# Router operations of a fused transformer block move from VectorE to GpSimd, with a softplus sum in halves and fills counted per unit

## The reference

```
h = layernorm(x) * (1 + ca) + sa
x = x + ga * A(h)          # A: attention (16 heads of 16) and a state-space scan side by side, then a feed-forward net
h = layernorm(x) * (1 + cb) + sb
x = x + gb * F(h)          # F: a linear layer plus routed LoRA experts
```

```
logits = x @ router_w.T + router_b                 # 8 experts
kth    = second largest logit
masked = where(logits < kth, -1e9, logits)
w      = softmax(masked)
out    = x @ base_w.T + base_b + 2.0 * sum_e w[e] * (x @ lora_A[e]) @ lora_B[e]
```

## Time and profile before

| | us |
|---|---|
| three runs | 5759.66, 5759.91, 5764.49 |
| median | 5759.91 |
| profiled execution, its own time | 5763.4 |
| its span, first to last instruction | 5761.6 |

### The profile page before, as it was taken

The page is one execution under the profiler, slowest core; times in us unless marked ns, Lnnn a source line. Parts: engine busy times, 40 slices in busy tenths (PEclk is TensorE's granted clock), DMA queues, the critical chain, the costliest instruction groups (busy, mean ns, idle before and its releaser), DMA issues.

```text
span 5761.6 us, 94560 instructions
## 1 busy us (share of the span) xinstructions
PE 5214.0 (90%) x32280; PEld 3490.0 (61%) x32280; DVE 5161.4 (90%) x7776; ACT 4082.5 (71%) x6407; POOL 4217.8 (73%) x2545
## 2 busy tenths in 40 slices
PE   4799998999999999999999999999999999999986
PEld 2466665666666566666566656666656666666664
DVE  4999999999999999999999999999999999999983
ACT  3777777767777777777777777777777777777763
POOL 3777777777777777777777777777777777777762
PEclk7899999999999999999999999999999999999998
DMA  4444445444444444444444445444454445554441
GB/s 127 145 146 140 146 143 147 146 148 133 151 136 153 143 145 140 145 142 154 142 143 138 142 150 151 143 138 143 143 155 147 142 139 146 143 151 145 140 128 39
DMA packets 521455, 812.22 MB, mean 141 GB/s; under 512 B 80432, under 2 KB 227288, under 8 KB 520976
## 3 DMA queue, kind: packets, MB, share of 16 engines
q1 hardware_dynamic: 513072, 805.79, 46.5%
q10 hardware_dynamic: 7904, 0.39, 0.1%
HBM read 716.50 MB, written 88.38 MB: 140 GB/s over the span
## 4 chain that ended last, share of the span: by engine, by line
PE 54%; DVE 22%; ACT 10%; issue 9%; DMA 1%; POOL 1%; SPq 1%; DVEq 0%; POOLq 0%; ACTq 0%
PE pY L931 8%; PE pM L1073 8%; PE pM L1082 7%; DVE pD L1192 6%; PE pM L953 4%; DVE state L1200 4%; PE pM L1062 4%; PE pM L1006 4%; DVE mx L1250 3%; PE pM L1037 3%; DVE xc L1232 3%; PE pM L1019 2%; PE pM L940 2%; PE pM L988 2%; DVE state L1192 2%
## 5 line engine op out<-in xcount | busy, mean ns | idle before, releaser
L575 POOL TENSOR_TENSOR state<-scan_in,bc 128x1024 f32<-128x1024 f32 x1024 | 2426.1, 2382 | 852.7 <-PE pY L931 603.1
L1192 DVE TENSOR_TENSOR_SCAN pD<-pD,state 128x512 f32<-128x512 f32 x1536 | 1830.0, 1215 | 111.9 <-ACT pD L699 96.8
L699 ACT ACTIVATE pD<-scan_in,A 128x512 f32<-128x512 f32 x2048 | 1391.7, 686 | 432.8 <-DVE state L1200 336.0
L931 PE MATMUL pY<-ident,state 128*128 128x128 f32 x8192 | 1180.7, 280 | 13.0 <-DVE state L1200 8.5
L931 PEld LDWEIGHTS pY<-ident,state 128*128 128x128 f32 x8192 | 934.9, 145 | 258.8 <-issue 178.3
L1200 DVE TENSOR_TENSOR state<-pD,bc 128x512 f32<-128x512 f32 x1536 | 1030.6, 682 | 23.6 <-DMA bc<-bc_d 8.7
L800 ACT ACTIVATE region<-pM 128x512 f32<-128x512 f32 (+1 forms) x1408 | 754.1, 555 | 329.6 <-PE pM L1039 303.9
L1250 DVE TENSOR_REDUCE mx<-pM 128x1 f32<-128x512 f32 (+3 forms) x1408 | 857.1, 628 | 122.0 <-PE pM L1021 119.5
L1037 PE MATMUL pM<-region 98*128 98x512 bf16 (+3 forms) x2048 | 559.8, 318 | 269.2 <-ACT region L800 149.8
L562 POOL TENSOR_TENSOR state<-state,bc 128x512 f32<-128x512 f32 x512 | 647.5, 1273 | 205.0 <-DVE state L1192 175.5
L1019 PE MATMUL pM<-region 96*128 96x512 bf16 (+3 forms) x2048 | 548.2, 305 | 92.9 <-DVE mx L1250 71.6
(11 more groups left out here) (171 smaller groups left out, 8359.8 us busy)
## 6 DMA issues: line engine op xcount, KB each, us to landing
bc<-bc_d SPq DMA_DIRECT2D x2048, 256.0 KB, 4.1
region<-qk_d SPq DMA_DIRECT2D x640, 128.0 KB, 3.6
qk_d<-qkp SPq DMA_DIRECT2D x64, 384.0 KB, 2.9
qk_d<-ht SPq DMA_DIRECT2D x64, 384.0 KB, 4.0
xt<-in_x_dram SPq DMA_DIRECT2D x32, 512.0 KB, 5.4
hres_d<-xt SPq DMA_DIRECT2D x32, 512.0 KB, 4.8
region<-qk_d SPq DMA_DIRECT2D x256, 64.0 KB, 3.1
x<-hres_d SPq DMA_DIRECT2D x32, 512.0 KB, 5.0
```

The source lines that it names most:

```text
L575: nc.gpsimd.tensor_tensor(state[:, at_:at_ + JP], us[:, parity(b), k // N * JP:(k // N + 1) * JP, :], bc[:, k % BC_SLOTS, 0, :].unsqueeze( ...
L699: act.activation(pD[DECAY_BANK[e]][:], dts[:, parity(b), j], ACT.Exp, scale=A[:, j, n:n + 1]).then_inc(a_ok.sem, 1)
L931: ins = pe.matmul(y_part(t, e % JP), state[:, e % RING, t * P:(t + 1) * P], ident[:], is_transpose=True, start=False, stop=(e % PASS >= PA ...
L1192: v.tensor_tensor_scan(h if e in POOL_C else decay, decay, h, 0.0, ALU.mult, ALU.add)\
```

## The change

1. **Router.** Three operations go to GpSimd as steps `route`, `wkeep` and `wnorm`, which stand behind `+ql2` and ahead of `fill18`: the subtraction of the largest logit (into a new tensor `lgs`), the product with `keep`, and the product with the reciprocal of the sum. The factor 2.0 goes into `lora_B` once, in the setup. `keep` stays on VectorE as four operations of 128x8 with the second largest logit as a scalar per partition. The sum and its reciprocal stay on VectorE as step `esum` between `scan31` and `lora`.
2. **Softplus sum** in halves, `sp3_0` and `sp3_1`, each with its count, so that `u0` waits for the first half only, and so does ScalarE's first decay.
3. **Fills** are counted per unit.
4. **Order of waits.** In `scan` the wait for the decay stands ahead of that for the fill; in `fill_states` that for TensorE comes first; ScalarE's `oe` waits for its buffer first; a second wait on the same semaphore in `mx` at its first step is gone.

Nothing else in the lists and in the placement of banks changes.

```diff
+        lgs = sb("lgs", [P, TB, E])
@@
-                    e = JP * last + JP - 1
                     if row == 0:
-                        before.wait(sp, b_ok, e + 1)
+                        before.wait(sp, b_ok, last + 1)
@@ fill_states
-                if k == 0:
-                    b.wait(pool, u_ok)
-                b.wait(pool, *row_in(b, k, 0))
-
                 if e >= RING:
                     b.wait(pool, y_ok, e + JP - RING)
                 else:
                     b.wait_last(pool, y_ok, SCANS + e + JP - RING)
+                if k % N == 0:
+                    b.wait(pool, u_ok, k // N + 1)
+                b.wait(pool, *row_in(b, k, 0))
...
-                                        ALU.mult).then_inc(b_ok.sem, JP)
+                                        ALU.mult).then_inc(b_ok.sem, 1)
@@ GpSimd
+                elif name == "route":
+                    b.wait(pool, rt_c)
+                    nc.gpsimd.tensor_tensor(lgs[:], lg[:], top[:, :, 0:1].broadcast_to([P, TB, E]), ALU.subtract)\
+                      .then_inc(rk_ok.sem, 1)
+                elif name == "wkeep":
+                    b.wait(pool, ex_ok)
+                    b.wait(pool, kp_ok)
+                    nc.gpsimd.tensor_tensor(ew[:], ew[:], keep[:], ALU.mult).then_inc(wk_ok.sem, 1)
+                elif name == "wnorm":
+                    b.wait(pool, es_ok)
+                    nc.gpsimd.tensor_tensor(ew[:], ew[:], esum[:].unsqueeze(2).broadcast_to([P, TB, E]), ALU.mult)\
+                      .then_inc(ew_ok.sem, 1)
@@ ScalarE, oe
-                    b.wait(act, pv_ok, (g + 1) * TB)
                     if g:
                         b.wait(act, ot_ps, g)
                     else:
                         b.wait_last(act, o_fin)
+                    b.wait(act, pv_ok, (g + 1) * TB)
@@ ScalarE, route2
-                    b.wait(act, rt_c)
-                    act.activation(ew[:], lg[:], ACT.Exp).then_inc(ex_ok.sem, 1)
+                    b.wait(act, rk_ok)
+                    b.wait(act, kp_ok)
+                    act.activation(ew[:], lgs[:], ACT.Exp).then_inc(ex_ok.sem, 1)
@@ VectorE
+            link(v.tensor_scalar(w_lb[:], w_lb[:], LORA_SCALE, None, ALU.mult))
@@ scan
-                b.wait(dve, b_ok, e + 1)
                 b.wait(dve, a_ok, e + 1)
+                b.wait(dve, b_ok, e // JP + 1)
@@ softplus
-                    v.tensor_tensor(dts[:, par], dts[:, par], us[:, par], ALU.add).then_inc(dt_ok.sem, 1)
+                    v.tensor_tensor(dts[:, par, half], dts[:, par, half], us[:, par, half], ALU.add)\
+                     .then_inc(dt_ok.sem, 1)
@@ route
-                    v.tensor_tensor(keep[:], lg[:], top[:, :, 1:2].broadcast_to([P, TB, E]), ALU.is_ge)\
-                     .then_inc(rt_c.sem, 1)
-                    b.wait(dve, rt_c, 6)
-                    v.tensor_tensor(lg[:], lg[:], top[:, :, 0:1].broadcast_to([P, TB, E]), ALU.subtract)\
-                     .then_inc(rt_c.sem, 1)
+                    for t in range(TB):
+                        v.tensor_scalar(keep[:, t, :], lg[:, t, :], top[:, t, 1:2], None, ALU.is_ge).then_inc(kp_ok.sem, 1)
+                elif name == "esum":
+                    b.wait(dve, wk_ok)
+                    v.tensor_reduce(esum[:], ew[:], AX_X, ALU.add).then_inc(es_ok.sem, 1)
+                    b.wait(dve, es_ok, 1)
+                    v.reciprocal(esum[:], esum[:]).then_inc(es_ok.sem, 1)
                 elif name == "lora":
-                    b.wait(dve, ex_ok)
-                    v.tensor_tensor(ew[:], ew[:], keep[:], ALU.mult).then_inc(ew_ok.sem, 1)
-                    b.wait(dve, ew_ok, 1)
-                    v.tensor_reduce(esum[:], ew[:], AX_X, ALU.add).then_inc(ew_ok.sem, 1)
-                    b.wait(dve, ew_ok, 2)
-                    v.reciprocal(esum[:], esum[:]).then_inc(ew_ok.sem, 1)
-                    b.wait(dve, ew_ok, 3)
-                    v.scalar_tensor_tensor(out=ew[:], in0=ew[:], scalar=LORA_SCALE,
-                                           in1=esum[:].unsqueeze(2).broadcast_to([P, TB, E]),
-                                           op0=ALU.mult, op1=ALU.mult).then_inc(ew_ok.sem, 1)
@@ ORDER
-POOL: ... fill17 +ql2 fill18 ...
+POOL: ... fill17 +ql2 -route -wkeep -wnorm fill18 ...
-DVE:  ... -route scan31 -lora ...      ... +mx0_1 +sp3 c58 ...
+DVE:  ... -route scan31 -esum -lora ...      ... +mx0_1 +sp3_0 +sp3_1 c58 ...
```

More of the change, by code:

```diff
@@ L423, in bc_row @@
                 if before.reg is not None or before.off >= 0:
-                    e = JP * last + JP - 1
                     if row == 0:
-                        before.wait(sp, b_ok, e + 1)
+                        before.wait(sp, b_ok, last + 1)
                     else:
-                        before.wait(sp, *product_after(e))
+                        before.wait(sp, *product_after(JP * last + JP - 1))
                 sp.dma_start(bc[:, slot, row], bc_d[b.index, k // N, row * N + k % N].partition_broadcast(P))\
@@ L608, in step @@
                     half = slice(int(name[1]) * J // 2, (int(name[1]) + 1) * J // 2)
-                    b.wait(pool, dt_ok)
+                    b.wait(pool, dt_ok, int(name[1]) + 1)
                     nc.gpsimd.tensor_tensor(us[:, par, half], dts[:, par, half], xc[:, half], ALU.mult)\
@@ L690, in decay @@
                 j, n = k // N * JP + e % JP, k % N
-                if e == 0:
-                    b.wait(act, dt_ok)
+                if e % PASS == 0:
+                    b.wait(act, dt_ok, e // PASS + 1)
                 scanned = (DECAY_BANK + DECAY_BANK[:e])[::-1].index(DECAY_BANK[e])
@@ L1235, in step @@
                             op0=ALU.mult, op1=ALU.add).then_inc(xs_c.sem, 1)
-                elif name == "sp3":
-                    par = parity(b)
+                elif name in ("sp3_0", "sp3_1"):
+                    par, half = parity(b), slice(int(name[4]) * JP, (int(name[4]) + 1) * JP)
                     b.wait(dve, dt_e)
-                    v.tensor_tensor(dts[:, par], dts[:, par], us[:, par], ALU.add).then_inc(dt_ok.sem, 1)
+                    v.tensor_tensor(dts[:, par, half], dts[:, par, half], us[:, par, half], ALU.add)\
+                     .then_inc(dt_ok.sem, 1)
                 elif name[:2] == "mx":
                     g, e = int(name[2]), int(name[4:])
-                    if e == 0:
-                        if g >= 2:
-                            b.wait(dve, s_ps, 12 * (g - 1))
-                        else:
-                            b.wait_last(dve, s_ps, 12 * (g + 3))
                     qb, heads = MAX_FILLS[e]
@@ L1345 @@
 MODS_DONE = MODS_READY + 1
[L1346 removed]
+DVE_SETUP = MODS_DONE + 13 + BANKS
 def parse(text):
@@ L1362 @@
         fill8 fill9 +l0s pc14 pc15 +l0a -f1_0 fill10 +l0b +l0c fill11 +l1s fill12 fill13 pc22 pc23 -x2 -x2b fill14
-        -l3s +ql0 fill15 +ql1 pc30 fill16 fill17 +ql2 fill18 -xb pc31 fill19 -gb -put fill20 pc38 fill21 pc39 fill22
-        fill23 fill24 +ql3 pc46 pc47 fill25 fill26 fill27 fill28 fill29 pc54 pc55 fill30 fill31 +u0 +u1 +fill0 pc62
-        pc63 +fill1 +fill2 +fill3 +fill4 +pc6 +fill5 +pc7 l2s +fill6 +fill7
+        -l3s +ql0 fill15 +ql1 pc30 fill16 fill17 +ql2 -route -wkeep -wnorm fill18 -xb pc31 fill19 -gb -put fill20
+        pc38 fill21 pc39 fill22 fill23 fill24 +ql3 pc46 pc47 fill25 fill26 fill27 fill28 fill29 pc54 pc55 fill30
+        fill31 +u0 +u1 +fill0 pc62 pc63 +fill1 +fill2 +fill3 +fill4 +pc6 +fill5 +pc7 l2s +fill6 +fill7
     """,
@@ L1397 @@
         mt0 scan22 scan23 -f2_0 mx1_0 scan24 scan25 c24 c25 -f2_1 scan26 c26 mx1_1 scan27 c27 mx1_2 +qk0 -l3s scan28
-        mx1_3 c28 +xs0 +qk1 scan29 scan30 +qk2 c29 +xs1 -route scan31 -lora scan32 scan33 mx1_4 c32 c33 +qk3 scan34
-        scan35 mx1_5 mx1_6 mx1_7 mx1_8 mx1_9 c34 mx1_10 c35 gate0 mt1 scan36 scan37 c36 mx2_0 c37 mx2_1 scan38 mx2_2
-        mx2_3 scan39 scan40 on0 c40 mx2_4 mx2_5 scan41 scan42 c41 c42 mx2_6 +xs2 scan43 scan44 c43 mx2_7 mx2_8 c44
-        mx2_9 mx2_10 scan45 mt2 c45 +xs3 on1 mx3_0 scan46 mx3_1 scan47 mx3_2 scan48 scan49 c48 mx3_3 mx3_4 c49 mx3_5
-        scan50 mx3_6 mx3_7 c50 scan51 mx3_8 c51 scan52 mx3_9 c52 scan53 mx3_10 c53 scan54 scan55 scan56 c56 mt3
-        scan57 scan58 +mx0_0 on2 c57 +mx0_1 +sp3 c58 scan59 c59 scan60 c60 scan61 c61 scan62 scan63 +scan0 +c0 on3
-        gate1 +scan1 +c1 +scan2 +scan3 +c2 +mx0_2 +c3 +scan4 +scan5 +c4 +c5 +scan6 +scan7 +scan8 +scan9 +c8 sso0 +c9
-        sso1 l2s +mx0_3 +mx0_4 +scan10 +scan11 +c10 +c11 +mx0_5 +mx0_6 +scan12 +scan13 +c12 +c13 +mx0_7
+        mx1_3 c28 +xs0 +qk1 scan29 scan30 +qk2 c29 +xs1 -route scan31 -esum -lora scan32 scan33 mx1_4 c32 c33 +qk3
+        scan34 scan35 mx1_5 mx1_6 mx1_7 mx1_8 mx1_9 c34 mx1_10 c35 gate0 mt1 scan36 scan37 c36 mx2_0 c37 mx2_1
+        scan38 mx2_2 mx2_3 scan39 scan40 on0 c40 mx2_4 mx2_5 scan41 scan42 c41 c42 mx2_6 +xs2 scan43 scan44 c43
+        mx2_7 mx2_8 c44 mx2_9 mx2_10 scan45 mt2 c45 +xs3 on1 mx3_0 scan46 mx3_1 scan47 mx3_2 scan48 scan49 c48 mx3_3
```

(5 more changed lines are left out.)

9 lines of the change are left out of this document (5 added, 4 removed).

## The result

| | us |
|---|---|
| before, beside the changed kernel, median of 7 | 5759.45 |
| after, median of 7 (5774.91 to 5789.58) | 5782.14 |
| ratio, 95% interval | 1.0042, 1.0031 to 1.0054 |
| after once more (e13), median of 9 | 5783.02, 1.0035 (1.0023 to 1.0048) |
| profiled execution of after, its span | 5789.58, 5787.8 |

The change costs 0.4%, some 23 us; no change was forecast, 5760.

A forecast was written before the change was run, and what follows sets the result against it. The prediction took TensorE and VectorE, each busy 90%, to bound the kernel in turn. Router -0.5 and setup +0.3 were counted as 0 on 5763.4 us profiled, 3.5 above the median: forecast 5760, range 5742 to 5783.

The forecast's parts named there:

- Keep runs free: Router on VectorE: four keep operations don't wait for GpSimd, 0.3 us together; the forecast case, chance 0.42.
- The rival that had it still waiting: Router on VectorE: keep operations still wait for GpSimd's port lock, 5776 to 5780 us; chance 0.23.
- T: The end of GpSimd's ql2 operation, from which the prediction timed the router's steps.
- The setup's 0.29 us against 0.43: Setup, 128x256: one-source operation 0.29 us, two-source 0.43; cited as a sign that keep may need the second port.
- The round trip, -0.5 us: Router steps through GpSimd and ScalarE and back to VectorE: 22 batches gain 0.34 us, 9 lose 0.78, together -0.5 us.
- B: Router pattern of some 9 batches: keep falls between two fills, the subtraction waits 2.28 us; forecast loss 0.78 us each.
- A: Router pattern of some 22 batches: keep itself waits for GpSimd's fills, about 2.2 us; forecast gain 0.34 us each.
- The softplus halves, 0: Softplus sum on VectorE in two operations of about 1.2 us: extra time covered by idle time, taken as 0.
- +2.4 if a fill slipped in: Softplus sum: upper bound of +2.4 us a batch if a GpSimd fill came between the halves.
- Clock comes back (faster): TensorE's L988 matmuls after the router in B: 1.27 us a batch back, 5748 or 5738 us; chance 0.20.
- Clock lost (slower): TensorE's L988 matmuls in A fall into the half-clock stretch: up to +20 us, 5780 us; chance 0.15.
- Order of waits, setup, `fill18`: Scan waits 0.07 us shorter, 1 us at most in all; one setup operation +0.3 us; GpSimd's fill18 delay hidden in A.

The follow-up runs named there:

- e13: The changed kernel itself measured once more, against the kernel before: 5783.02 us, ratio 1.0035.
- e5: Kernel before with only keep as four one-source operations of 128x8, nothing moved to GpSimd: 5781.02 us, ratio 1.0038.
- e8: Changed kernel with keep as one operation reading logits from PSUM and the softplus sum in one operation: 5769.54 us, ratio 1.0016.
- e18: e8 repeated: 5771.14 us, ratio 1.0025.
- e10: e8 with scan32 ahead of esum on VectorE and an attention exponential ahead of the router's on ScalarE: 5765.82 us, ratio 1.0007.
- e1: Changed kernel with the whole router as in the kernel before; halves, fill counts and order of waits stay: 5760.29 us, ratio 1.0001.
- e2: Changed kernel with the softplus sum in one operation again: 5771.01 us, ratio 1.0019.
- e7: Kernel before with the scan's wait for the decay written ahead of the one for the fill: 5760.23 us, ratio 1.0004.
- e11: e8 with GpSimd multiplying by keep twice, lengthening the round trip: 5763.88 us, ratio 1.0009.

## Why the prediction was wrong

- **"Keep runs free": wrong.** The rival that had it still waiting described the trace: last `keep` at T + 0.36 (0.1 to 0.35 said), scan32 at T + 2.80 (2.7 to 2.95), 953 ns for each. In the Trainium skill, "VectorE: DVE Perf Modes", section "The perf-mode tier table", gives fp32 `tensor_scalar` from SBUF to SBUF double rate through both read ports. The runs agree that such an operation is held, also for eight elements: e5 shows it alone. The sentence was read, and its rival given 0.23 against 0.42. The price of `keep` was taken from the three MAX8, which run free beside the fills though they read SBUF; this didn't carry over to `tensor_scalar`. The setup's 0.29 us against 0.43 was a sign for two elements a cycle.
- **The round trip, -0.5 us: this is the term that fails also without the lock.** Prices were right: GpSimd 0.24 to 0.25 us (0.26 said), exponential at T + 0.24 in e8 (0.26), LoRA product where `keep` is free at T + 1.65 (1.69), scan32 at T + 2.26 (2.30), and the router stretch on VectorE 2.6 and 3.5 us shorter in e8 and e18. The failed step is "in B it gets later by about as much as VectorE does, and I count it once", with A's 0.34 us of VectorE taken as a gain. TensorE isn't released there by VectorE alone but by ScalarE's attention exponentials, which got later in A as well, and the time is lost behind scan32. Priced by that end, the prediction's own numbers give 22 x 0.2 + 9 x 1.3 = 16 us; e8 and e18 measured 9 and 14. The later release is in the traces. That it is the cause of the 9 to 14 us stays open: e10 takes the stall away and is not clearly faster.
- **The softplus halves, 0: mis-sized.** The bound "+2.4 if a fill slipped in" was the mechanism and the size; it happens in 0 to 4 of 32 batches, 4 us in the mean of four executions. With the old router the halves cost nothing measurable (e1), with the new one 11 (after against e2).
- **Clock comes back (faster): this came true, at the place that was named.** The four matmuls of L988 (L1005 in after) take over 2.7 us in 8 batches before and in 3, 2, 2 and 3 in the four executions of after, and scan40 to scan44 is 8.5 to 10 us shorter. **Clock lost (slower):** not at L988 but at the router itself, behind the stall of TensorE, in 4 to 6 batches of 1.1 us. Together the clock gives back more than it takes in these executions, so, as far as one trace of before can tell, it is no part of the 23 us.
- **Order of waits, setup, `fill18`:** as forecast, nothing that can be measured (e1, e7).

That 5782 lies in the stated range is luck: its upper end came from the slower rivals, and the forecast's own range ended at 5769.

The sum is not closed. The new router with its lock measures 11 us (e2), the halves' 4 us make 15, and after shows 21 to 23. e2's interval reaches up to 16 us, those of after down to 18 and, in e13, 13, so the 7 us left are about as large as their uncertainty. Why the halves cost 11 us only where `keep` is held as well is open beyond these 4. Nor is it settled whether e11, with the longer trip, is faster than e8.

## What to carry to other kernels

Before work moves from a busy engine to another to get round a shared port, look for an operand that can lie in PSUM: here the same operations fell from 1585 and 1355 ns to 191 without a hand-over. Ask of each engine in a detour which work stands behind the moved step on it, and price the step by the engine that is released last. An operation that is split can be separated by another engine's instruction; look at when that one starts, and by what, before the split is taken as free. And a wait that grows in one trace is not yet a price: compare it over several executions of the same kernel.
